# Routed experts: from a dense pass over all eight to tokens sorted into blocks of 128 slots

## The reference

```python
scores = softmax(xf @ gate_w.T)                  # (2048, 8)
topk_w, topk_i = top_k(scores, 2)                # two experts per token
topk_w = topk_w / sum(topk_w)
cw = zeros_like(scores).at[arange(T)[:, None], topk_i].add(topk_w)
g, u = einsum('th,ehi->eti', xf, wg), einsum('th,ehi->eti', xf, wu)   # 8 experts, 256 -> 128
eo = einsum('eti,eih->eth', silu(g) * u, wd)                          # 128 -> 256
y = einsum('te,eth->th', cw, eo)
shared = silu(xf @ sg) * (xf @ su) @ sd                               # 256 -> 256 -> 256
x = layernorm(xf + y + shared)
```

## Time and profile before

| | us |
|---|---|
| median of 3 runs (798.22 to 799.35) | 798.26 |
| span of the profiled execution | 798.3 |
| layer 1's attention ends, first expert matmul starts | 546.9 |
| last down matmul ends | 792.3 |
| TensorE busy in the span | 743.9 (93%) |
| VectorE, ScalarE, GpSimd busy | 402.3, 395.3, 174.3 |

### The profile page before, as it was taken

The page is one execution under the profiler, slowest core; times in us unless marked ns, Lnnn a source line. Parts: engine busy times, 40 slices in busy tenths (PEclk is TensorE's granted clock), DMA queues, the critical chain, the costliest instruction groups (busy, mean ns, idle before and its releaser), DMA issues.

```text
span 798.3 us, 10995 instructions
## 1 busy us (share of the span) xinstructions
PE 743.9 (93%) x3831; PEld 332.2 (42%) x3831; DVE 402.3 (50%) x984; ACT 395.3 (50%) x519; POOL 174.3 (22%) x194
## 2 busy tenths in 40 slices
PE   5998889999989789897999999989999999999996
PEld 2656222224323535342222222324466457448345
DVE  1578225334767787965133333465432842652525
ACT  1245858886778153453888888773121130120110
POOL 0012534443232222145244223231200200000000
PEclk9997789999999799999899999999999999999999
DMA  8401242332220000022444555470000000000000
GB/s 278 120 0 30 54 82 37 53 56 37 40 38 1 1 0 14 0 40 49 79 81 82 83 83 83 78 200 1 0 1 0 28 0 1 26 0 0 26 1 27
DMA packets 32276, 36.15 MB, mean 45 GB/s; under 512 B 7956, under 2 KB 21009, under 8 KB 32065
## 3 DMA queue, kind: packets, MB, share of 16 engines
q1 hardware_dynamic: 32217, 35.41, 21.7%
HBM read 12.54 MB, written 2.10 MB: 18 GB/s over the span
## 4 chain that ended last, share of the span: by engine, by line
PE 65%; DVE 13%; SPq 10%; ACT 5%; issue 4%; DMA 2%; POOL 1%; DVEq 0%; ACTq 0%; POOLq 0%
PE ps L2109 17%; PE ps L1303 13%; PE ps L1286 11%; PE ps L2134 9%; ACT probs L1373 3%; SPq L1024 3%; PE ps L1683 3%; SPq L999 2%; SPq L1031 2%; PE ps L400 2%; DVE stats L291 1%; PE ps L649 1%; PE ps L1670 1%; DVE raw L1206 1%; PE ps L2119 1%
## 5 line engine op out<-in xcount | busy, mean ns | idle before, releaser
L1373 ACT ACTIVATE probs<-ps 128x1024 f32<-128x1024 f32 (+1 forms) x320 | 276.0, 965 | 66.2 <-PE ps L1286 66.0
L1286 PE MATMUL ps<-ops_mem 99*128 99x512 bf16 (+3 forms) x768 | 167.5, 340 | 13.5 <-issue 6.7
L1303 PE MATMUL ps<-probs,vstat 128*32 128x512 f32 (+3 forms) x1536 | 168.9, 513 | 9.2 <-DVE raw L1206 7.4
L2109 PE MATMUL ps<-ops_mem,parts_mem 128*128 128x512 f32 x320 | 147.1, 605 | 1.0 <-DVE probs L2161 1.0
L1389 POOL TENSOR_SCALAR_AFFINE_SELECT probs<-probs 128x512 f32<-128x512 f32 x128 | 84.8, 663 | 223.1 <-ACT probs L1373 222.4
L1286 PEld LDWEIGHTS ps<-ops_mem 99*128 99x128 bf16 x768 | 58.1, 99 | 166.5 <-ACT probs L1373 86.1
L1206 DVE COPY raw<-ps 128x512 f32<-128x512 f32 x32 | 22.1, 691 | 167.4 <-PE ps L1303 167.2
L2055 ACT ACTIVATE ops_mem<-ps 128x512 f32<-128x512 f32 x40 | 23.9, 597 | 142.9 <-PE ps L2109 142.9
L2109 PEld LDWEIGHTS ps<-ops_mem,parts_mem 128*128 128x128 f32 x320 | 58.9, 191 | 68.4 <-issue 66.0
L2134 PE MATMUL ps<-parts_mem,probs 128*128 128x256 f32 x320 | 70.5, 380 | 0.0
L2134 PEld LDWEIGHTS ps<-parts_mem,probs 128*128 128x128 f32 x320 | 60.3, 190 | 8.4 <-issue 0.5
(11 more groups left out here) (191 smaller groups left out, 723.6 us busy)
## 6 DMA issues: line engine op xcount, KB each, us to landing
ops_mem<-parts_mem SPq DMA_DIRECT2D x276, 64.0 KB
ops_mem<-parts_mem SPq DMA_DIRECT2D x66, 32.0 KB
yT<-in_xT SPq DMA_DIRECT2D x4, 512.0 KB, 7.9
xres<-in_x SPq DMA_DIRECT2D x1, 2048.0 KB, 14.6
out<-ops_mem SPq DMA_DIRECT2D x3, 512.0 KB, 2.9
rope<-in_rope SPq DMA_DIRECT2D x1, 1024.0 KB, 6.8
parts_mem<-in_wg SPq DMA_DIRECT2D x2, 512.0 KB, 5.0
parts_mem<-in_wu SPq DMA_DIRECT2D x2, 512.0 KB, 6.9
```

The lines of the kernel that those rows point to most:

```text
L1286: last = nc.tensor.matmul(ps[:, bank, o:o + CH - lo], kT[0:KDIM, buf, h if kh == GH else 0, kt * P:(kt + 1) * P], qT[0:KDIM, buf, h, c * C ...
L1303: last = nc.tensor.matmul(ps[32 * h:32 * h + 32, AV, lo:CH], vstat[:, i % 2, kt, h if kh == GH else 0, :], probs[:, s % PRING, h, 0:CH - l ...
L1373: nc.scalar.activation(o, banks, ACT.Exp, scale=score_scale).then_inc(s_exp, 1)
L2109: last = nc.tensor.matmul(ps[:, 4 + 2 * (e % 2) + m, :], w, xT[:, kk, :], start=kk == 0, stop=kk == 1)
```

## The change

The shared expert stays dense. For the routed experts, per batch of 1024 tokens:

- Two routing constants and two HBM buffers are new. `x_slots` has 23 blocks x 128 slots x 256 f32 per batch, and SP fills it with zeros right behind the input loads. The same holds for `o_slots`, without the fill.
- Chunks 0 and 1 are projected in item 4 of layer 1's attention, turned in items 5 and 6, their logits made and experts chosen in item 6. In item 7 TensorE counts ranks with nine small bf16 matmuls and VectorE works out each choice's slot. Chunk 2 is projected in item 7. GpSimd issues batch 0's 16 indirect scatters (128 rows of 1 KB each) between the masks of item 7 and behind them.
- In the tail, four of eight shared gate/up groups, chunk 3's projection, the transposes, the logits and two shared down products come first. Then 46 units (2 batches x 23 blocks) run. Each unit turns a block of 128 slots, multiplies it by one expert's gate and up (256 columns in one), turns the hidden values and multiplies by down. The expert's number is read from SBUF into a TensorE register, four at a time, and selects the weights' place. The unit's output goes to `o_slots`.
- GpSimd issues batch 1's scatters, then, when all of a batch's outputs are stored, its 16 indirect gathers. VectorE adds each gathered row times its gate to the token's sum. Batch 0's sums are placed beside units 28 to 43, batch 1's behind the last unit, beside the other shared work. All three pieces of the last norm follow the last sum.

The core of the diff:

```diff
-NE = EXPERTS + 2
+SHARED = 2
+BLOCKS = (2 * T + EXPERTS * (P - 1)) // P
+UNITS = NB * BLOCKS
+PER_LOAD = 4
+STORES = 4
...
+            for slot_rows in x_slots:
+                sp.dma_start(slot_rows.rearrange("(u p) n -> u (p n)", p=P), a["no_rows"].to_broadcast([BLOCKS, P * C])
+                             ).then_inc(s_route_c, 16)
...
+            def rank(self, pe, b):
...
+                nc.tensor.matmul(at, below, ones, start=True, stop=False)
+                for d in range(1, TPB + 1):
+                    last = nc.tensor.matmul(at[:, EXPERTS * d:], every, ones[:, 0:EXPERTS * (TPB + 1 - d)],
+                                            start=False, stop=d == TPB)
...
+            def scatter(self, pool, b, lo, hi):
+                if lo == 0:
+                    pool.wait_ge(self.s_slots, b + 1)
+                for n in range(lo, hi):
+                    k, t = n % 2, n // 2
+                    nc.gpsimd.indirect_dma_start(
+                        out=x_slots[b], in_=xres[:, b * TPB + t, :], in_offset=None,
+                        out_offset=bass.IndirectOffsetOnAxis(ap=slots[:, b, TPB * k + t:TPB * k + t + 1], axis=0)
+                    ).then_inc(self.s_scattered[b], 16)
...
+                        if layer == 1 and i == NI - 1 and d >= 3:
+                            behind.scatter(pool, 0, *((0, 4), (4, 5), (5, 6), (6, 7), (7, 9))[d - 3])
...
+                def bring(b):
+                    for r in range(STORES):
+                        loaded(pool, SLOT_LOADS[r], len(range(r, (b + 1) * BLOCKS, STORES)))
+                    for t in range(TPB):
+                        for k in range(2):
+                            nc.gpsimd.indirect_dma_start(
+                                out=returned[b][:, t, k, :], out_offset=None, in_=o_slots[b],
...
+                late.scatter(pool, 1, 0, 2 * TPB)
+                take_slots(nc.gpsimd, 1)
+                pool.wait_ge(s_turned, BLOCKS)
+                bring(0)
+                bring(1)
...
+                for u in range(UNITS):
+                    gates_of(u)
+                    if u >= 1:
+                        turn_h(u - 1)
+                    if u + 2 < UNITS:
+                        turned(u + 2)
+                    if u >= 2:
+                        product(u - 2)
+                    if u == 1:
+                        late.rank(pe, 1)
+                    if (u + 2) % BLOCKS % PER_LOAD == 0 and u + 2 < UNITS:
+                        expert_load(u + 2)
+                gate_up(4, (0,))
+                turn_h(UNITS - 1)
+                product(UNITS - 2)
+                gate_up(4, (1,))
+                product(UNITS - 1)
+                for q in range(5, 7):
+                    gate_up(q)
+                down(2)
+                gate_up(7)
+                down_last()
...
+                    r = u - BLOCKS - 5
+                    if 0 <= r < 2 * TPB and r % 2 == 0:
+                        add_back(0, r // 2)
```

More of the change, by code:

```diff
@@ L403, in project_y @@
             last.then_inc(s_proj, 1)
[L405 to L426, removed]
+        GATE_COUNT, ROUTE_COUNT = 11, 8
@@ L495, in shift @@
[L495 to L512, removed]
+                k = self.count(dve, 1)
@@ new lines, in between @@
+            def between(self, dve, i):
+                if i == 4:
+                    for m in range(2):
+                        for half in range(2):
+                            self.sum(dve, m, half)
+                if i == 5:
+                    self.of.scale()
+                    self.apply(0, 0)
+                    self.apply(1, 1)
+                    self.keep_xT(dve, 0, 0)
+                if i == 6:
+                    self.shift(dve, 0)
+                    for _ in self.choose(dve, 0):
+                        pass
+                if i == 7:
+                    for half in range(2):
+                        self.sum(dve, 2, half)
@@ L1166, in _, with attention @@
                     pe.wait_ge(ops.s_shifted, 2)
-        def attention(layer, ops, first, banks_free, buffer_free, gates=None, finish=None, ahead=None):
+        def attention(layer, ops, banks_free, buffer_free, finish=None, ahead=None, behind=None):
             kh = KEYS_OF[layer]
@@ L1224, in _ @@
                 for i in range(NI):
-                    if layer == 1 and i == NI - 2:
-                        first.sum(dve)
                     if layer == 0 and i == NI - 1:
@@ L1257, in _ @@
                         ahead.second_apply(norm)
-                    if layer == 1 and i == NI - 1:
-                        first.apply()
-                        gates.first_x(dve, first.s_norm)
-                        gates.first_xT(dve)
+                    if behind:
+                        behind.between(dve, i)
                     take(dve, i, 1)
@@ L1268, in _ @@
                         ahead.norm(dve)
-                    if layer == 1 and i == NI - 2:
-                        first.norm(dve)
+                    if behind:
+                        behind.after(dve, i)
             @on("tensor")
@@ L1379, in _ @@
                 for i in range(NI):
-                    if layer == 1 and i == NI - 2:
-                        pool.wait_ge(s_y, NI)
-                        pool.wait_ge(s_vstat[layer], NI // 2)
-                        for g in range(NG // 2):
-                            first.stage(g, 0)
                     for d, s in enumerate(DIAG):
@@ new lines, in expert_load @@
+                def expert_load(u):
+                    b, j = u // BLOCKS, u % BLOCKS
+                    pe.wait_ge(late.s_expert, b + 1)
+                    hi = min(j + PER_LOAD, BLOCKS)
+                    _, found = nc.values_load_multi_w_load_instructions(
+                        expert_at[:, b, j:hi], engines=[mybir.EngineType.PE], min_val=0, max_val=EXPERTS - 1,
+                        skip_runtime_bounds_check_because="a count of passed experts, cut off at the last one")
+                    for n, e in enumerate(found):
+                        expert[u + n] = e
@@ new lines, in _, with weight, gates_of @@
+                expert = {}
+                def weight(u, part):
+                    return w_routed[:, bass.ds(expert[u] * WROW + part * C, C)]
+                def gates_of(u):
+                    pe.wait_ge(s_xg, u + 1)
+                    if u < 2:
+                        pe.wait_ge(s_hs, 4)
+                    else:
+                        pe.wait_ge(s_h, u - 1)
+                    for kk in range(2):
+                        last = nc.tensor.matmul(ps[:, 2 + u % 2, 0:C], xgT[:, u % 3, kk, :], weight(u, kk),
+                                                start=kk == 0, stop=kk == 1)
+                    last.then_inc(s_pre, 1)
```

855 lines of the change are left out of this document (531 added, 324 removed).

## The result

The changed kernel takes **928.8 us** (median of 4 runs, 922.41 to 929.93) against 798.48 (4 runs, 798.22 to 799.35): ratio 1.161, 95% interval 1.158 to 1.165. It is slower by 130 us. The forecast was 733. What happened is rival 1: the fills of zeros ran on one DMA engine.

A forecast was written before the change was run, and what follows sets the result against it. TensorE was taken to bound the replaced expert stage. After 546.9 us the terms 10 + 35 + 97.6 + 4.2 + 24 + 15.5 sum to 186.3 against 251.4, giving 733 us; own range 700 to 785, with rival 1 700 to 930.

The forecast's parts named there:

- rival 1: Zero fills behind the input loads run on one DMA engine, first scores 190 us later, 923 us in all; chance 0.27.
- hidden, 0 us: The two zero fills, 6.0 MB, spread over 16 engines in 16 us, or 30 at half rate, costing nothing.
- 1 layer 1's attention, more: Layer 1's attention grows by 10 us from added projections, transposes, logits and rank matmuls on TensorE; bounds 0 and 15.
- 2 until the first unit: From attention's end to the first unit, 35 us: shared matmuls, chunk 3's projection, transposes, logits, and 5 us of waiting.
- 3, 4 units and shared halves: Expert loop: 46 units at 2.1 us plus 1 for the second rank, 97.6; shared half-groups between the last units, 4.2.
- 5, 6 behind the last unit: After the last unit: copy, store, 16 gathers and landing, 24 us; then additions, three norms and store, 15.5.
- Term 3: Expert loop: 46 units at 2.1 us each, plus 1 us for the second rank, 97.6 us.
- the 0.3 us per group of matmuls: In each unit, 0.3 us for its groups on top of 1.62, taken from the dense stage's 245 against 231 us.
- the 1 us per register read: In the unit loop, expert numbers read into registers once per four units at 1 us, 0.2 us per unit.
- rival 3: GpSimd's queue sets the expert stage's pace at 2.4 us per indirect DMA, 762 us in all; chance 0.11.
- rival 2: Units run at half clock or the engines' pace, 3.3 us each, 55 us more, 788 us in all; chance 0.13.
- Term 5: After the last unit: copy, hand-over, store, 16 gathers at 1.2 us (19.2) and landing, 24 us in all.

The follow-up runs named there:

- e8: e6 with the norms of the first batch's two chunks both formed behind the expert loop: 737.78 us, 0.925 of the kernel before.
- e6: e1 with GpSimd clearing a 128x128 tile before each of batch 1's scatters and all gathers, and first-batch sums four units later: 742.32 us (0.930).
- e12: e8 with 128x256 cleared before the second batch's scatters and first batch's gathers, and returned rows added one unit later: 726.90 us (0.909).
- e1: The changed kernel with both zero fills written as 16 rows of 184 KB instead of 23 of 128 KB: 763.86 us (0.955).
- e3: The kernel before with only the two fills of 23 rows of 128 KB added behind its first loads: 966.93 us (1.211).
- e4: e1 with the second batch's 16 scatters issued one per unit of the expert loop instead of back to back: 754.84 us (0.946).
- e13: e1 with the second batch's 16 scatters replaced by 16 plain stores of the same 128 KB tiles: 748.23 us, one run.
- e9: e1 with eight buffers instead of four for the units' results on their way to the slot buffer: 767.05 us (0.961).
- e5: The kernel before with 16 indirect scatters in a row in the dense pass, into a buffer nobody reads: 801.41 us (1.004).
- e11: The changed kernel with its 23-row fills issued on GpSimd's queue at the start instead of SP's: 859.01 us (1.076).

## Why the prediction was wrong, step by step

**The fills: the step that failed.** The text took them at "hidden, 0 us" and named them the largest open term. They cost 172.7 us up to the first scores. From there to layer 1's first scores the kernel was 6.7 us shorter than before; without a late fill this stretch took 290.3 to 294.7 us (e8, e6, e12, e1, before), and the kernel before with the fill (e3) took 290.3, so part of it is a spread between executions and the rest stays unexplained. Rival 1 had the mechanism in full. Its number, 923, came out near 928.8 partly by luck: the engine moved 27 to 33 GB/s instead of the 24 that was divided out of the earlier trace rows, so the delay was 173 and not 190; these 17 us and the 6.7 were made up by a layer 1 and an expert stage 27 us over the sum (table below). The weight was wrong, not the list. Three rows on three engines at share 0.20 was the only row that bore on it and spoke for the rival; nothing spoke for the forecast but the wish that long rows be cut otherwise. The Trainium skill's rule ("DMA: Bandwidth & Descriptors", section "Why a DMA increments its semaphore by 16 and not by 1": the largest number up to 16 that divides the slowest dimension of both sides) agrees with all three counts that were run: shares of 0.07, 0.13 and 1.04 for 23, 46 and 16 rows.

**The terms of the stage**, predicted against measured, in the changed kernel and in e12:

| term, us | predicted | changed | e12 |
|---|---|---|---|
| 1 layer 1's attention, more | 10 | 9.1 | not split off |
| 2 until the first unit | 35 | 37.8 | not split off |
| 3, 4 units and shared halves | 101.8 | 119.5 | 85.3 |
| 5, 6 behind the last unit | 39.5 | 46.7 | 44.6 |
| sum | 186.3 | 213.1 | |

Terms 1 and 2 hold within 3 us. Term 3 was wrong in both directions. A unit costs 1.62 us, the bare column sum, and not 2.1: the 0.3 us per group of matmuls and the 1 us per register read (some 12 reads) cost nothing that can be seen. The 0.3 came from a check with a slip: 3.63 us for eight records are 0.45 each, not 0.43, and over 40 groups that is half of the 14 us left over. (Another slip without effect: the last of the ten slices in the earlier trace rows shows 6 tenths, not 9.) Against that stands the stall, for which the sum had no term: "keep pace", the text said of the gathers, and it asked of GpSimd's queue only how long it takes. The interval was right (1.27 against 1.2), so rival 3 is refuted; what a full queue does to the others was not asked. The clock adds to it: a unit's four gate records take 1.03 us at full clock, and 2.07 at 783.72 us, where the granted clock had fallen to 0.50 while TensorE stood. That is as far as rival 2 is right. Two norms that VectorE does between two units (848.6 to 854.0 and 866.8 to 872.3 us) held the loop up by some 3.5 us each; the sum had them at nothing because VectorE has room on the mean. e6 moved the second behind the loop and e8 the first as well, for 4.5 us.

**Term 5.** Sixteen gathers at 1.25 us (group mean 947 ns) took 19.7 us, as forecast. The extra 7 us are the stalled shared expert: its Silu waited 17.9 us, and half a norm, eight additions and the last norms queued behind it on VectorE.

**The whole.** Without the fill's fault the change does what it was forecast to do in kind, but less: 763.9 (e1) where 733 stood, 31 us short. Spacing (with one norm moved) gave 21.5 of them back (e6), 26 with both norms moved (e8), 37 with the wider spacing (e12). All versions with the fill on sixteen engines are faster than the kernel before.

**What stays open**: by which path an indirect transfer of GpSimd slows the other engines. Shown are the spacing (e4, e6, e12), that bytes don't do it (e13) and that store buffers don't matter (e9); the indirect form itself rests on one run with a shorter row (e13), and why the dense pass is spared (e5) is open. A cause inside the chip is not shown by any run.

## What to carry to other kernels

Give the outer dimension of every large DMA 16 rows, or another count that 16 divides (of the row counts only 16, 23 and 46 were run here), and check its DMA share in the trace. One engine of 16 looks like an idle chip, and the transfers behind it wait, also those of another queue (e11). Don't let GpSimd issue indirect transfers back to back beside a loop with many short hand-overs; put other work, or an idle 0.3 us, between them. When a term of zero is the largest open one, give its rival the weight that the only row near it supports.

## What the runs showed of the hardware that was not expected

- A copy from HBM to HBM of 23 rows ran on one DMA engine at 27 to 33 GB/s, one of 46 rows on two at 56, one of 16 rows on sixteen at 378.
- While the fills ran on one engine, SP needed 9.60 us for an issue of two transfers that took 1.24 us in the kernel before, and 67.69 us for a single small load. With the fills on GpSimd's queue, the issue of one input load on SP's took 104.87 us.
- The same two 23-row fills ran on one engine from SP's queue (share 0.07, 29 GB/s) and on two from GpSimd's (0.12, 53 GB/s).
- An indirect DMA of 128 rows of 1 KB occupies GpSimd for 0.95 to 0.97 us, and the next starts 0.30 us later, scatter or gather. Sixteen plain stores of the same size took 8.60 us, 0.54 each.
- Beside a row of indirect DMAs at 1.27 us, after the first five or six, single waits of ScalarE, VectorE and TensorE in the unit loop grew to 3 to 9 us (TensorE busy 8.24 of 20 us), and the last shared Silu waited 17.94; at 1.57 us between them TensorE was busy 24.00 of 24 us. In the dense pass the row at 1.27 us left TensorE as it was (20.59 of 21 us).
- Matmuls whose weight address comes from a register, four expert numbers read every fourth unit, lost no time by it: 1.62 us from unit to unit for 9 records.
